# Split products reordered into three parts over all their blocks, each part with its own wait

## What is computed

```
x = x + rms(attention0(x, masked)) * scale0 * (1 + sc(c)) + shift(c)      # layer 0
x = x + attention1(g1(c) * rms(x) + b1(c))                                # layer 1
x = x + (silu(z @ gate.T) * (z @ hid.T)) @ out.T,   z = g2(c) * rms(x) + b2(c)
```

## Time and profile before

| | |
|---|---|
| median of 3 runs | 324.95 us (324.79 to 325.38) |
| the profiled execution | 326.49 us, of which its span is 324.7 us |
| TensorE matmuls busy | 315.1 us, 97% of the span, 5016 matmuls |
| VectorE, ScalarE, GpSimd busy | 238.2 us, 204.5 us, 181.4 us |
| mean granted TensorE clock | 0.995 |

### The profile page before, as it was taken

One profiled execution on the slowest core, in us unless ns is written; L12 is line 12 of the kernel. 1 busy time (PEld: TensorE's weight loads), 2 busy tenths in 40 slices (PEclk: granted clock), 3 DMA queues, 4 the chain that ended last, 5 costly groups with the idle time before them and its releaser, 6 DMA issues.

```text
span 324.7 us, 11938 instructions
## 1 busy us (share of the span) xinstructions
PE 315.1 (97%) x5016; PEld 297.6 (92%) x5016; DVE 238.2 (73%) x425; ACT 204.5 (63%) x445; POOL 181.4 (56%) x207
## 2 busy tenths in 40 slices
PE   7989999999989999999999999999999999999996
PEld 6869878899989999999999999998999999999995
DVE  4796769896997898796959598798963783554344
ACT  3787587989884577588475765685572466333231
POOL 7296798334767376468651766479280653553310
PEclk9997999999999999999999999999999999999999
DMA  7955841304000300300003000100000100000010
GB/s 228 302 151 138 249 150 34 101 2 134 2 3 2 99 2 2 101 35 2 4 0 102 32 6 0 36 0 5 0 3 2 35 32 2 2 10 25 2 34 33
DMA packets 11238, 17.08 MB, mean 53 GB/s; under 512 B 1328, under 2 KB 5440, under 8 KB 11184
## 3 DMA queue, kind: packets, MB, share of 16 engines
q1 hardware_dynamic: 11008, 15.80, 16.0%
q0 software_dynamic: 176, 0.51, 0.7%
HBM read 14.14 MB, written 2.16 MB: 50 GB/s over the span
## 4 chain that ended last, share of the span: by engine, by line
PE 80%; DVE 6%; POOL 4%; DMA 3%; issue 3%; ACT 2%; DVEq 0%; POOLq 0%; ACTq 0%
PE ps L1589 62%; PE ps L1712 5%; PE ps L1694 5%; DMA w_stage<-in_weights 3%; PE ps L1745 3%; DVE row_max L1140 2%; PE ps L1777 2%; DVE probs L1148 2%; PE ps L1730 1%; PE ps L1682 1%; POOL w_lo L411 1%; POOL x_row L422 1%; PE ps L1756 1%; ACT probs_T L713 1%; DVE mod_tile L1183 0%
## 5 line engine op out<-in xcount | busy, mean ns | idle before, releaser
L1589 PE MATMUL ps<-ff_hi,w_hi 128*128 128x256 f32 x256 | 72.9, 285 | 0.9 <-DVE ff_lo L1221 0.9
L1589 PE MATMUL ps<-ff_lo,w_hi 128*128 128x256 f32 x256 | 72.1, 282 | 0.0
L1589 PE MATMUL ps<-ff_hi,w_lo 128*128 128x256 f32 x256 | 72.1, 281 | 0.0
L474 POOL TENSOR_TENSOR h_lo<-w_stage,h_hi 128x512 fp32r<-128x512 f32 x29 | 37.4, 1291 | 43.6 <-ACT h_hi L769 43.6
L468 POOL TENSOR_TENSOR probs<-probs,inv_row 128x512 f32<-128x512 f32 x40 | 41.3, 1051 | 34.2 <-DVE inv_row L1161 34.2
L1589 PEld LDWEIGHTS ps<-ff_hi,w_hi 128*128 128x128 f32 x256 | 48.2, 188 | 1.5 <-issue 1.0
L1140 DVE TENSOR_REDUCE row_max<-ps 128x8 f32<-128x512 f32 x64 | 40.8, 680 | 10.6 <-PE ps L1694 10.4
L1589 PEld LDWEIGHTS ps<-ff_hi,w_lo 128*128 128x128 f32 x256 | 48.2, 188 | 0.0
L1589 PEld LDWEIGHTS ps<-ff_lo,w_hi 128*128 128x128 f32 x256 | 48.2, 188 | 0.0
L706 ACT ACTIVATE probs<-probs 128x512 f32<-128x512 f32 x64 | 38.8, 634 | 11.2 <-DVE probs L1148 10.9
L1234 DVE SCALAR_TENSOR_TENSOR w_stage<-w_stage,ps 128x512 f32<-128x512 f32 x32 | 21.7, 677 | 30.4 <-ACT w_stage L762 30.3
(11 more groups left out here) (111 smaller groups left out, 825.2 us busy)
## 6 DMA issues: line engine op xcount, KB each, us to landing
w_stage<-in_weights SPq DMA_DIRECT2D x20, 256.0 KB, 4.7
mod_tile<-mod_rows_dram SPq DMA_DIRECT2D x32, 128.0 KB, 3.2
x_T<-in_xT SPq DMA_DIRECT2D x8, 256.0 KB, 3.3
x_row<-in_x SPq DMA_DIRECT2D x8, 256.0 KB, 2.8
out<-x SPq DMA_DIRECT2D x7, 256.0 KB, 2.1
x<-in_cond POOLq DMA_DIRECT2D x1, 392.0 KB, 6.5
out<-x SPq DMA_DIRECT2D x2, 128.0 KB, 1.9
x<-in_rows POOLq DMA_DIRECT2D x1, 96.0 KB, 6.3
```

What stands on the lines that cost most here:

```text
L474: pool.tensor_tensor(h_lo[q % 2][:], h_T[q % 2], h_hi[q % 2][:], ALU.subtract)\
L1589: mm = pe.matmul(dst, x, y, start=first and n == 0, stop=last and n == len(terms) - 1, skip_group_check=True)
```

## The change

The three terms are no longer issued pair by pair. `products` issues one part, say high by high, for all pairs of both blocks, and is called three times. The term with the low part that is made last comes at the end, and in front of each part stands the wait for what it needs: first the operand's high part (and the weights' high part in chunk 0), then the weights' low part, at the end the operand's low part. `queries` and `values` have no wait for their operand, since `keys` of the same chain has waited. The waits for the bank's readers stay ahead of the first matmul. The number of matmuls and their operands stay; `first_keys` becomes `keys(0)`, with the same order as before. The queues of the other engines and the order of TensorE's list are untouched.

```diff
--- before.py
+++ after.py
@@ -1583,12 +1583,20 @@
                 for s, count in readers:
                     pe.wait_ge(s, count)
 
-            def split_product(dst, pairs, first=True, last=True):
-                terms = [(x[i], y[j]) for x, y in pairs for i, j in ((0, 0), (0, 1), (1, 0))]
-                for n, (x, y) in enumerate(terms):
-                    mm = pe.matmul(dst, x, y, start=first and n == 0, stop=last and n == len(terms) - 1,
-                                   skip_group_check=True)
+
+
+            BOTH_HIGH, SECOND_LOW, FIRST_LOW = (0, 0), (0, 1), (1, 0)
+
+            def products(blocks, part, closing=False):
+
+                for dst, pairs, opens in blocks:
+                    for n, (x, y) in enumerate(pairs):
+                        mm = pe.matmul(dst, x[part[0]], y[part[1]], start=opens and part == BOTH_HIGH and n == 0,
+                                       stop=closing and n == len(pairs) - 1, skip_group_check=True)
                 return mm
+
+            def weight_hi(name):
+                return weight_hi_of(W_ORDER.index(name))
 
             def warm_up():
 
@@ -1611,61 +1619,50 @@
                                    condT, start=True, stop=True)
                 mm.then_inc(modT_mm, 1)
 
-            def project_features(a, name, bank):
-                for m in range(KT):
-                    mm = split_product(ps[:, bank, TC * m:TC * m + TC],
-                                       [(w_parts(name, k, P * m, P), (in_hi[a % NS][:, k, :], in_lo[a % NS][:, k, :]))
-                                        for k in range(KT)], first=m == 0)
-                return mm
+            def features(a, name, bank):
+                return [(ps[:, bank, TC * m:TC * m + TC],
+                         [(w_parts(name, k, P * m, P), (in_hi[a % NS][:, k, :], in_lo[a % NS][:, k, :])) for k in range(KT)],
+                         m == 0) for m in range(KT)]
 
             def keys(a, *readers):
                 c, l = CHAINS[a]
+                blocks = features(a, f"k{l}", K_BANK[a])
+                if c == 0:
+                    pe.wait_ge(*weight_hi(f"k{l}"))
+                pe.wait_ge(in_hi_ready, a + 1)
+                bank_free(*readers)
+                products(blocks, BOTH_HIGH)
                 if c == 0:
                     pe.wait_ge(*weight(f"k{l}"))
+                products(blocks, FIRST_LOW)
                 pe.wait_ge(in_lo_ready, a + 1)
-                bank_free(*readers)
-                project_features(a, f"k{l}", K_BANK[a]).then_inc(k_ready, 1)
-
-            def first_keys():
-
...
             def queries(a, *readers):
                 c, l = CHAINS[a]
+                blocks = features(a, f"q{l}", Q_BANK[a])
+                if c == 0:
+                    pe.wait_ge(*weight_hi(f"q{l}"))
+                bank_free(*readers)
+                products(blocks, BOTH_HIGH)
+                products(blocks, SECOND_LOW)
                 if c == 0:
                     pe.wait_ge(*weight(f"q{l}"))
-                bank_free(*readers)
-                project_features(a, f"q{l}", Q_BANK[a]).then_inc(q_ready, 1)
+                products(blocks, FIRST_LOW, closing=True).then_inc(q_ready, 1)
 
             def values(a, *readers):
                 c, l = CHAINS[a]
+                blocks = [(ps[:, V_BANK[a], D * t:D * t + D],
+                           [((in_hi[a % NS][:, k, P * t:P * t + P], in_lo[a % NS][:, k, P * t:P * t + P]),
+                             w_parts(f"v{l}", k, 0, D)) for k in range(KT)], t == 0) for t in range(NT)]
+                if c == 0:
+                    pe.wait_ge(*weight_hi(f"v{l}"))
+                bank_free(*readers)
+                products(blocks, BOTH_HIGH)
+                products(blocks, FIRST_LOW)
                 if c == 0:
                     pe.wait_ge(*weight(f"v{l}"))
-                bank_free(*readers)
-                for t in range(NT):
-                    rows = slice(P * t, P * t + P)
-                    mm = split_product(ps[:, V_BANK[a], D * t:D * t + D],
-                                       [((in_hi[a % NS][:, k, rows], in_lo[a % NS][:, k, rows]),
-                                         w_parts(f"v{l}", k, 0, D)) for k in range(KT)], first=t == 0)
-                mm.then_inc(v_ready, 1)
+                products(blocks, SECOND_LOW, closing=True).then_inc(v_ready, 1)
 
             def scores(a, *readers):
 
@@ -1758,15 +1755,19 @@
 
             def output_product(a, *readers):
                 c, l = CHAINS[a]
+                blocks = [(ps[:, Y_BANK[a], D * t:D * t + D],
+                           [((o_hi[a % 2][:, t, k, :], o_lo[a % 2][:, t, k, :]), w_parts(f"o{l}", k, 0, D)) for k in range(KT)],
+                           t == 0) for t in range(NT)]
+                if c == 0:
+                    pe.wait_ge(*weight_hi(f"o{l}"))
+                pe.wait_ge(o_hi_ready, a + 1)
+                bank_free(*readers)
+                products(blocks, BOTH_HIGH)
                 if c == 0:
                     pe.wait_ge(*weight(f"o{l}"))
+                products(blocks, SECOND_LOW)
                 pe.wait_ge(o_lo_ready, a + 1)
-                bank_free(*readers)
-                for t in range(NT):
-                    mm = split_product(ps[:, Y_BANK[a], D * t:D * t + D],
-                                       [((o_hi[a % 2][:, t, k, :], o_lo[a % 2][:, t, k, :]), w_parts(f"o{l}", k, 0, D))
-                                        for k in range(KT)], first=t == 0)
-                mm.then_inc(y_ready, 1)
+                products(blocks, FIRST_LOW, closing=True).then_inc(y_ready, 1)
 
             def transpose_normed(a, *readers):
                 pe.wait_ge(xs_ready, a + 1)
@@ -1778,42 +1779,54 @@
                 mm.then_inc(xsT_ready, 1)
 
             def hidden_in(k, j, *readers):
-                if k == 0 and j % 4 == 0:
-                    for name in (f"g{j // 4}", f"g{2 + j // 4}", f"h{j // 4}", f"h{2 + j // 4}"):
-                        pe.wait_ge(*weight(name))
+                blocks = [(ps[:, GU_BANK[k][j], TC * n:TC * n + TC],
+                           [(w_parts(name, kt, P * j, P, HID), (ff_hi[k % 2][:, kt, :], ff_lo[k % 2][:, kt, :]))
+                            for kt in range(KT)], n == 0) for n, name in enumerate(("gate", "hid"))]
+                loads = (f"g{j // 4}", f"g{2 + j // 4}", f"h{j // 4}", f"h{2 + j // 4}") if k == 0 and j % 4 == 0 else ()
+                for name in loads:
+                    pe.wait_ge(*weight_hi(name))
+                pe.wait_ge(ff_hi_ready, k + 1)
+                bank_free(*readers)
+                products(blocks, BOTH_HIGH)
+                for name in loads:
+                    pe.wait_ge(*weight(name))
+                products(blocks, FIRST_LOW)
                 pe.wait_ge(ff_lo_ready, k + 1)
-                bank_free(*readers)
-                for n, name in enumerate(("gate", "hid")):
-                    mm = split_product(ps[:, GU_BANK[k][j], TC * n:TC * n + TC],
-                                       [(w_parts(name, kt, P * j, P, HID), (ff_hi[k % 2][:, kt, :], ff_lo[k % 2][:, kt, :]))
-                                        for kt in range(KT)], first=n == 0)
-                mm.then_inc(gu_ready, 1)
-
-            def hidden_times_out(dst, q, j, t, first):
+                products(blocks, SECOND_LOW, closing=True).then_inc(gu_ready, 1)
+
+            def out_block(bank, q, j, t, opens):
                 rows = slice(P * t, P * t + P)
-                return split_product(dst, [((h_hi[q % 2][:, j % 2, rows], h_lo[q % 2][:, j % 2, rows]),
-                                            w_parts("out", j, 0, D))], first=first, last=j == NJ - 1)
+                return (ps[:, bank, D * t:D * t + D],
+                        [((h_hi[q % 2][:, j % 2, rows], h_lo[q % 2][:, j % 2, rows]), w_parts("out", j, 0, D))], opens)
 
             def hidden_out(k, j, *readers):
                 q = 4 * k + j // 2
-                if k == 0 and j % 2 == 0:
+                blocks = [out_block(ACC_BANK[k] if k < NCH - 1 else LAST_ACC_BANK[t], q, j, t,
+                                    j == 0 and (t == 0 or k == NCH - 1)) for t in range(NT)]
+                load = k == 0 and j % 2 == 0
+                if load:
+                    pe.wait_ge(*weight_hi(f"u{j // 2}"))
+                pe.wait_ge(h_hi_ready, q + 1)
+                bank_free(*readers)
+                products(blocks, BOTH_HIGH)
+                if load:
                     pe.wait_ge(*weight(f"u{j // 2}"))
+                products(blocks, SECOND_LOW)
                 pe.wait_ge(*hidden_lo_of(q))
-                bank_free(*readers)
-                for t in range(NT):
-                    bank = ACC_BANK[k] if k < NCH - 1 else LAST_ACC_BANK[t]
-                    mm = hidden_times_out(ps[:, bank, D * t:D * t + D], q, j, t, j == 0 and (t == 0 or k == NCH - 1))
-                mm.then_inc(h_used, 1)
```

(35 more changed lines are left out.)

1 line of the change is left out of this document (added).

## The result

The changed kernel takes 323.68 us (median of 20 runs, 322.79 to 326.59) where the kernel before takes 325.36 (20 runs, 323.71 to 327.32): ratio 0.996, 95% interval 0.9941 to 0.9978. A second timing of it gave 323.70 us and 0.996 again. The profiled execution took 323.21 us with a span of 321.4, so 3.3 us less than the one before.

What follows compares the result with a forecast made beforehand. TensorE, busy for 315.1 of 324.7 us, was taken as the bound, so only its stalls for low parts could be won. Terms 0.58 + 0.1 + 0.3 + 0.35 = 1.3 us off 324.95 gave 323.65 us, range 322.5 to 325.0.

Steps and rivals of the forecast that it cites:

- Part 1: All split products: the same matmuls in another order, some 770 added switches between bank halves, cost nothing; 0 us.
- The rival of alternating halves: Every product: switching bank halves costs up to 0.0055 us each; 325.85 us, at most 327.9; chance 0.12.
- the rule of the Trainium skill on bank cycling: Cycling through PSUM banks each iteration lets TensorE idle often enough for its clock to oscillate; time would end above before.
- The clock rival: Half-speed stretch from 26.4 to 29.8 us may go, taken as 1.0 us more gain: 322.65 us; chance 0.12.
- Part 2: About 180 added waits, mostly for high parts, are already satisfied when reached and cost nothing; 0 us.
- (a): queries(0), values(0): stalls of about 0.6 us go, but VectorE waits for weights to land anyway; worth 0.
- (b): keys(2): its 1.34 us stall is filled, VectorE gains 0.69 us, weigh_values(0) starts earlier; 0.58 us let through.
- the rival of absorption: Between 26 and 97 us a wait with a fixed end takes back the early gain; 324.3 us, or 324.6; chance 0.22.
- (c): output_product(1): 0.3 us stall goes, but transpose_output(2) needs VectorE, busy without a gap; worth 0.
- (d): hidden_in(0, 0): 1.02 us stall goes, mostly given back at transpose_probs(6, 1); 0.23 left, 0.1 us counted.
- (e): hidden_out(4, 6): 0.21 us stall and 0.10 restart go; 0.3 us.
- (f): The end, hidden_out(7, 4): 0.25 us stall and 0.10 restart go; 0.35 us directly on the end.

Runs made afterwards that it cites:

- order_lean: Kernel before with all split products in the three-part order, but exactly the old waits, all ahead of the first term: 325.48 us, ratio 1.0014.
- waits_only: Kernel before in its old order, with the added waits put between the matmuls of its products: 325.42 us, ratio 1.0016.
- order_only: Kernel before with every split product in three parts, but all waits, those for high parts too, ahead of its first matmul: 326.45 us, ratio 1.0046.
- hin00_only: Kernel before with hidden_in(0, 0) alone in three parts with their own waits: 325.27 us, ratio 0.9988.
- stream_plus20: Kernel before with a finer warm-up that puts 20 more instructions ahead of all else: 327.01 us, ratio 1.0058.
- start_only: Kernel before with the change for projections and output products of the first three chains alone: 324.68 us, ratio 0.9984.
- rest_only: Changed kernel with projections and output products of the first three chains as in the kernel before: 324.15 us, ratio 0.996.
- late_only: Kernel before with three parts and their own waits only from hidden_out(4, 6) on: 324.46 us, ratio 0.9977.
- stream_shifted: Kernel before with a finer warm-up, as long as the old one, that puts 112 more instructions ahead of all else: 335.05 us, ratio 1.0279.

## Why the prediction was right, and where only its sum was

The forecast was 323.65 us, the median is 323.68, and its side, "faster", holds. That the two lie 0.03 us apart is luck: the kernel before took 325.36 us beside it and not the 324.95 that the forecast set out from, so the medians part by 1.7 us and not by 1.3. The steps carry the result in unequal measure.

**Part 1, the order, 0.** Right: order_lean is at 1.0014 with 1 inside its interval, and the mean steps are those of the kernel before to 0.2 ns. They can't be told better: the changed kernel itself has 115.8 ns for the projections in one profile and 116.3 in the other, 0.4 us over their 768 matmuls. The rival of alternating halves did not come about. Nor did the rule of the Trainium skill on bank cycling that the prediction cites: the half-speed stretch is 3.40 us in both profiles (23.9 to 27.3 us in the changed kernel, 26.4 to 29.8 in the earlier trace rows). The clock rival did not come about either. By the mean granted clock of the timed executions (0.998 or more: no such stretch), 10 of 32 of the changed kernel are without it, and 50 of 102 of the kernel before. In the kernel before those without it take 325.08 us on average and those at 0.993 to 0.995 take 325.73, so the stretch goes with 0.65 us more, less than the 1.0 that the rival gave it.

**Part 2, the added waits, 0.** Right for the wait as such (waits_only 1.0016). But "a satisfied wait costs nothing" left out that a second wait ahead of one matmul can be an instruction, and that instructions move the block ends. In the changed kernel it is 4 instructions, and no pause of over 0.3 us was seen in its two profiles; in order_only it is 121, and the two pauses of its profile (1.4 us from start to start) are the size of its 0.0046.

**(a) 0 for queries(0).** The reason given, that weights land too late for it to matter, read one execution's late landing as the kernel's. In the changed kernel's profile scores(0) ends at 12.00 us, and the first maxima start at 12.24, without a gap behind VectorE's own w_lo. So the 0 holds there too, but because VectorE's list is full. In two of the profiles with the old start, hin00_only and stream_plus20, VectorE does wait for scores(0), by 0.20 and 0.13 us: so much (a) could be worth in some executions. The expectation of start_only, that the maxima start straight behind scores(0) in the changed kernel, is not what its rows show.

**(b) 0.58** (by its own numbers 26.14 - 25.55 = 0.59). The mechanism is in the trace: keys(2) without its 1.34 us, VectorE's 0.69 down to 0.21, and modulate_features directly ahead of weigh_values(0), which starts at 24.01 us and not 26.14.
```profile
22.06 1.92 PE L1617 MATMUL ps<-x 64*128 64x32 f32 x16
24.01 2.04 PE L1727 MATMUL ps<-v_pairs,probs_T 128*32 128x34 f32 x128
```
Most of these 2.13 us are the late landing. The other profiles take it out: weigh_values(0) starts at 23.86 to 24.27 us in the five with the new start, and at 24.53 to 25.39 in the seven with the old one and no late landing, 0.84 us apart on average. At the last matmul of values(8), ahead of hidden_in(0, 0), the means are still 0.6 us apart (93.7 and 94.3), but the two groups overlap. That speaks for a gain that is kept; each profile is one execution, though. In time the term is not settled: start_only gives 0.5 us with an interval that holds 0, and rest_only does without it. Whether the early gain is taken back, as the rival of absorption had it, stays open.

**(c) 0.** Right: transpose_output(2) now waits 0.29 us for o_row, on VectorE.

**(d) counted 0.1.** Mis-sized. The stall of 1.02 us went, 1.09 with the restart, and the give-back came at the named place, but it is 0.44 us there; 0.2 to 0.6 us stay in the four profiles (hin00_only 0.9988, an interval that holds 0.1 us as well). The step that failed is that the hidden groups "hang on GpSimd and VectorE, not on TensorE", so that hidden(0, 2) ends as before: the second and third tanh hung on TensorE's hidden_in, and the chain came 0.26 us closer behind the squares. With 0.23 it makes the 0.5 us that were to be had. Counting 0.1 of 0.23 was caution without a row; ahead of transpose_probs(6, 1) the four profiles give back another 0.1 to 0.3 us, and behind it up to 0.2.

**(e) 0.3 and (f) 0.35.** Right: hidden_out(4, 6) comes 0.31 us sooner against its predecessors (restart included) and the end 0.36 more, in the changed kernel and in late_only and rest_only alike. late_only's 0.9977 is 0.75 us for 0.65.

So 1.3 us were predicted and 1.3 to 1.7 measured, made of some 0.4 for (d), 0.7 for (e) and (f) and an early part between 0 and 1, where the prediction has 0.1 + 0.65 + 0.58. If the early part is 0, as the times of rest_only have it, the sum came out because (b) and (d) were off in opposite directions, which would be luck; if it is 0.6, as the profiles have it, (d) alone was too small.

## What to carry to other kernels

Putting the terms that need the late operand last is worth the stalls that it covers, where no other engine holds the same path; each must be followed to the next wait, and that can lie 10 us on, on another engine. When a chain is said to hang on other engines, check every link of it for the one that moves: here it was the second one. Add waits so that each rides on a weight load of its own. Before a difference under 1% is put down to an idea, look for pauses inside bursts at the ends of TensorE's blocks of 256 instructions, and for block ends that come under 3 us behind their packet, since an edit that only changes the number of instructions ahead of them can be worth more than the edit under test. One profile's DMA landings are one execution's; look at a second before a term is set to zero by them.

## What the runs showed of the hardware that was not expected

- TensorE pauses at the ends of its instruction blocks: eleven times for 0.5 to 2.2 us from start to start in four kernels, all at the same place of a block, 2.2 to 3.1 us behind the start of a 16 KB packet of instructions. 112 more instructions ahead made the kernel 2.8% slower, 20 more 0.6%.
- The half-speed stretch was 3.4 us in the kernel before and 10.2 us in stream_shifted, which paused for 2 us inside it. In order_only and start_only none was recorded there. Half of the timed executions of the kernel before have it and half do not; those that have it take 0.65 us longer on average.
- The weight load ahead of a matmul carried one wait: 178 more waits were 4 more instructions in the changed kernel and 121 in order_only.
- The same block of weights landed at 9.3 us in one execution and at 13.0 in another.
